# First attention of a fused attention and FFN kernel: next scores ahead of the values, a PSUM bank for the state sums, fewer dummy matmuls

## The reference

```
x = x + attention(layernorm(x), ctx, ctx)      # 16 heads of 32
x = x + ffn(layernorm(x))                      # 4-bit weights, 512 -> 2 x 1408 -> 512

# attention, per head: gates from [q, k, v]
log_D[s, t] = F[s] - F[t] + i[t]   for t <= s  # F: running sum of log-sigmoids
D  = exp(log_D - max_t log_D)
C  = (q @ k.T / sqrt(32)) * D
Cn = C / (max(|sum C|, exp(-max log_D)) + eps)
h  = Cn @ v, then normalized over the 32 of the head and scaled
```

## Time and profile before

| What | us |
|---|---|
| Median of 3 runs | 548.03 |
| Lowest and highest | 546.9, 548.43 |
| Profiled execution, its own time | 549.5 |
| Its span, first to last instruction | 547.8 |
| TensorE matmul busy | 507.3 (93%) |
| VectorE busy | 391.2 (71%) |
| GpSimd busy | 332.2 (61%) |
| ScalarE busy | 295.1 (54%) |
| Mean granted TensorE clock | 0.984 |

### The profile page before, as it was taken

The page is one execution under the profiler, slowest core; times in us unless marked ns, Lnnn a source line. Parts: engine busy times, 40 slices in busy tenths (PEclk is TensorE's granted clock), DMA queues, the critical chain, the costliest instruction groups (busy, mean ns, idle before and its releaser), DMA issues.

```text
span 547.8 us, 8218 instructions
## 1 busy us (share of the span) xinstructions
PE 507.3 (93%) x2752; PEld 280.2 (51%) x2752; DVE 391.2 (71%) x691; ACT 295.1 (54%) x639; POOL 332.2 (61%) x371
## 2 busy tenths in 40 slices
PE   0989996899999899999999999999999989989996
PEld 0556773436666345466665445566664443323442
DVE  4877878978888988277778898477778763877301
ACT  0355854387776352677767234787764224865000
POOL 1054446188887763667776883667768653888501
PEclk9988997999999999999999999999999999999999
DMA  8854037073103200456006001571000000200000
GB/s 270 245 175 167 9 109 256 33 258 136 40 2 134 97 0 2 130 186 225 0 7 227 0 1 41 193 269 39 2 1 1 19 20 25 90 1 1 20 19 38
DMA packets 22234, 47.81 MB, mean 87 GB/s; under 512 B 1840, under 2 KB 8880, under 8 KB 21680
## 3 DMA queue, kind: packets, MB, share of 16 engines
q1 hardware_dynamic: 22192, 47.28, 25.1%
HBM read 37.31 MB, written 4.33 MB: 76 GB/s over the span
## 4 chain that ended last, share of the span: by engine, by line
PE 73%; DVE 12%; ACT 5%; issue 4%; POOL 4%; DMA 1%; DVEq 0%; POOLq 0%; ACTq 0%
PE pf L993 25%; PE pf L979 18%; PE po L917 9%; PE pq L883 7%; PE pq L842 2%; PE pq L895 2%; PE pq L979 2%; PE pf L1012 2%; PE pq L922 2%; DVE ffn L1258 2%; ACT dmat L664 2%; DVE ffn L1262 1%; POOL hT L540 1%; ACT ts L698 1%; DVE bst L1081 1%
## 5 line engine op out<-in xcount | busy, mean ns | idle before, releaser
L993 PE MATMUL pf<-w_down,hT 128*128 128x512 f32 x352 | 154.0, 595 | 1.7 <-DVE w_down L1326 1.7
L979 PE MATMUL pf<-yT,gu_val 128*128 128x512 f16 x552 | 133.5, 380 | 4.5 <-DVE ffn L1262 1.7
L535 POOL TENSOR_TENSOR ffn<-ffn,ts 128x512 f32<-128x512 f32 x88 | 118.3, 1345 | 28.7 <-DVE ffn L1262 18.7
L698 ACT ACTIVATE ts<-pf,gu_scale 128x512 f32<-128x512 f32 x138 | 87.3, 684 | 46.8 <-PE pf L979 45.6
L993 PEld LDWEIGHTS pf<-w_down,hT 128*128 128x128 f32 x352 | 65.8, 190 | 83.8 <-issue 77.3
L979 PEld LDWEIGHTS pf<-yT,gu_val 128*128 128x128 f16 x552 | 49.9, 98 | 67.8 <-DVE ffn L1262 8.3
L664 ACT ACTIVATE dmat<-negm,aT 128x128 f32<-128x128 f32 x248 | 77.7, 396 | 0.8 <-DMA negm<-negm_dram 0.8
L540 POOL TENSOR_TENSOR hT<-ffn,th 128x512 f32<-128x512 f32 x44 | 57.7, 1314 | 28.9 <-DVE th L1271 28.9
L1258 DVE SCALAR_TENSOR_TENSOR ffn<-pf,gu_scale,ts 128x512 f32<-128x512 f32 x69 | 51.6, 748 | 32.7 <-PE pf L979 18.7
L917 PEld LDWEIGHTS po<-v_sb,dmat 128*128 128x128 f32 x512 | 62.1, 192 | 4.8 <-issue 0.4
L494 POOL TENSOR_SCALAR_AFFINE_SELECT dmat<-dmat 128x512 f32<-128x512 f32 x64 | 44.2, 705 | 27.1 <-ACT dmat L664 27.1
(11 more groups left out here) (124 smaller groups left out, 650.9 us busy)
## 6 DMA issues: line engine op xcount, KB each, us to landing
negm<-negm_dram SPq DMA_DIRECT2D x31, 512.0 KB, 5.2
ffn<-in_x SPq DMA_DIRECT2D x4, 1024.0 KB, 6.7
xT<-in_ctx_T SPq DMA_DIRECT2D x16, 256.0 KB, 6.0
ctx_sb<-in_ctx SPq DMA_DIRECT2D x4, 1024.0 KB, 5.7
x_sb<-in_x SPq DMA_DIRECT2D x4, 1024.0 KB, 5.5
x_res<-x_sb SPq DMA_DIRECT2D x4, 1024.0 KB, 5.4
out<-x_res SPq DMA_DIRECT2D x16, 256.0 KB, 2.2
ts<-in_gate_up_bytes SPq DMA_DIRECT2D x4, 352.0 KB, 9.5
```

Source lines behind the costliest of these rows:

```text
L535: pool.tensor_tensor(acc, acc, ts[:, h % TDEEP, 1], ALU.add).then_inc(tsum_ready, 1)
L698: act.activation(ts[:, h % TDEEP, g], bank(q, h, g), ACT.Copy, scale=gu_scale[:, g * GU + o:g * GU + o + 1]).then_inc(t_ready, 1)
L979: last = pe.matmul(bank(q, h, g), gu_val[:, h // 2 + h % 2 * FT, g], yT[:, part, g], start=(part == 0), stop=(part == 1))
L993: last = pe.matmul(pf[:, tt], hT[:, j, tt * P:(tt + 1) * P], w_down[:, j], start=(j == 0), stop=(j == FT - 1))
```

## The change

In the first attention, and only there:

- The second half of the next unit's scores is put directly behind the first half, both ahead of the values. The dummies that stood between the first half and the values are gone (six with unit 0, three with each of units 1 to 6). Those behind the state sums stay.
- The state sums of pair 0 go to `pf` bank 1, columns 0 to 131 (`bank_state`); the later part stays in `pq` bank 1. State sums now wait for `keep_state` of the unit before (`state_ready`), and the matmul L922 waits for the later part of the unit before (`later_ready`).
- On VectorE the later part of unit u is taken behind keep_state of unit u+1 (that of unit 7 at h = 17), ahead of the decode step.

```diff
+        def bank_state(p):
+            return pf[:, 1] if p == 0 else pq[:, 1]
...
                 pe.wait_ge(vw_ready, 2 * UNITS * p + 2 * u + 2)
-                if u > 0:
+                if p == 0:
+                    if u > 0:
+                        pe.wait_ge(state_ready, u)
+                elif u > 0:
                     pe.wait_ge(later_ready, UNITS * p + u)
                 elif q is not None:
                     pe.wait_ge(t_ready, 4 * FT * q + 2)
-                pe.matmul(pq[:, 1, 0:HG * (DH + 1)], ctx_sb[:, 2 * b, hg * P:(hg + 1) * P],
+                pe.matmul(bank_state(p)[:, 0:HG * (DH + 1)], ctx_sb[:, 2 * b, hg * P:(hg + 1) * P],
...
+                if p == 0 and u > 0:
+                    pe.wait_ge(later_ready, u)
                 pe.wait_ge(state_ready, UNITS * p + u + 1)
...
                         if q is None and s in VALUES and VALUES[s] + 1 < UNITS:
                             scores(p, q, VALUES[s] + 1, 0)
-                            if VALUES[s] == 0:
-                                keep_busy(6, po[:])
-                            else:
-                                keep_busy(3)
+                            scores(p, q, VALUES[s] + 1, 1)
                         if s in VALUES:
                             values(p, q, VALUES[s])
                             if q is None and VALUES[s] + 1 < UNITS:
-                                scores(p, q, VALUES[s] + 1, 1)
                                 state_sums(p, q, VALUES[s] + 1)
                                 keep_busy(6 if VALUES[s] == 0 else 3)
...
-                dve.tensor_tensor(state[:, u % 2], pq[:, 1, 0:HG * (DH + 1)].rearrange(
+                dve.tensor_tensor(state[:, u % 2], bank_state(p)[:, 0:HG * (DH + 1)].rearrange(
...
                     if u is not None and q is None:
                         products(p, u, range(BLKS))
                         keep_state(p, u)
+                        if u > 0:
+                            later_part(p, u - 1)
+                    if q is None and s - 1 in VALUES and VALUES[s - 1] == UNITS - 1:
+                        later_part(p, UNITS - 1)
...
-                    if p is not None and s in VALUES:
+                    if p is not None and q is not None and s in VALUES:
                         later_part(p, VALUES[s])
```

## The result

| | before | after |
|---|---|---|
| Median, us | 548.23 (546.9 to 548.55, 4 runs) | 563.22 (562.31 to 564.0, 4 runs) |
| Profiled execution, us | 549.5 | 562.63 |
| Span, us | 547.8 | 560.9 |
| Mean granted clock | 0.984 | 0.944 |

The ratio is 1.0278, with a 95% interval of 1.0252 to 1.0303: slower by 15.0 us. The forecast was 562, slower.

A forecast was written before the change was run, and what follows sets the result against it. TensorE's queue was taken to bound the first attention. First turn -3.4, full-clock units -0.6, five half-clock units +17.2 and the end about nothing gave +13, so 562 us; range 542.5 to 567, the forecast's own 554 to 567.

The forecast's parts named there:

- What bounds the loop, and the clock: First attention: TensorE's queue sets the pace at 5.12 us a unit; 3.9 us without dummies make its clock fall.
- unit 2 or 3: First attention loop: the units in which TensorE's clock was expected to fall to 1.2 GHz.
- The first turn, -3.4: Loop entry: products of unit 2 start at 46.9 in place of 50.33, a gain of 3.4 us.
- Units at half clock, 8.56: First attention loop: TensorE's unit takes 8.56 us at 1.2 GHz with values doubled, 3.44 more than now.
- B: First attention loop: the clock falls and comes back by turns; 549 to 554, say 551 us; chance 0.22.
- C: First attention loop: clock falls and stays at 1.2 GHz until the sixteen dummies behind unit 7; 562 us, chance 0.42.
- The end, "at about nothing": Loop end: the last unit's dummies and the end together change the time by about nothing.
- the sum: First attention: first turn -3.4, one or one and a half full-clock units -0.6, five half-clock units +17.2, end about nothing: +13.
- A: First attention loop: the clock holds at 2.4 GHz, -5.5 us; 544.0 profiled, 542.5 on the median; chance 0.28.
- VectorE's unit of 4.6: First attention, VectorE: products, state, decode, add and later part take 4.6 us a unit, without the 0.46 wait.
- D: First attention loop: scores ahead bring nothing, VectorE waits for state sums or weighted values; 545 to 549, say 548; chance 0.08.

The follow-up runs named there:

- run 4: Kernel before, with the 36 loop dummies from unit 1 on replaced by float32 matmuls of 33 columns: 571.58 us, ratio 1.0444.
- run 10: Kernel before, plus only eight dummies in TensorE's idle gap ahead of the first FFN products: 548.01 us, ratio 0.9998.
- run 1: Changed kernel with the removed dummies back, behind the second half of the scores (six with unit 0, three with units 1 to 6): 548.07 us, ratio 1.0005.
- run 5: Changed kernel with five dummies a unit: one between the score halves, two behind them, two behind the state sums (six with unit 0): 546.92 us, ratio 0.9983.
- run 2: Kernel before, old order and bank, only the dummies between first half of scores and values removed: 566.01 us, no ratio given.
- run 8: Kernel before, order and dummies kept, only the state sums' bank and the later part's place on VectorE changed: 548.89 us, ratio 1.0016.

## Why the prediction was right

**What bounds the loop, and the clock.** TensorE's queue set the pace and stayed the bound. The clock fell as the text had it, after a long time without a dummy (the first time at 40.7, earlier than its unit 2 or 3), and run 4 showed that it is narrow work in a full queue that loses it. The rule of the Trainium skill that was weighed (TensorE: Matmul & The Clock Gate, "Why this matters for your kernels"), that mid-kernel drops come with idle gaps, does not cover this case: the measurement decides, by 9.98 of 10.0 us busy ahead of the fall in run 4.

**The first turn, -3.4.** Products of unit 2 start 8.4 us behind those of unit 0, where 46.9 against 38.56 was 8.3. The size was right and its cause only in part: 1.6 of it was the half clock of the profiled execution of before, which not every execution has (run 10). At full clock the distance went from 10.15 to 8.63 (run 1) or 8.46 (run 5). As a gain over the median, 3.4 was about twice too much. This is probably the larger part of why run 1 came out at 548.07 and not at 546.

**Units at half clock, 8.56.** Measured 8.32: scores 2.45 (2.40 in the text), values 3.55 (3.42), L930 0.60 (0.62), state sums 0.44 (0.84), dummies 1.28. Doubling the values was right. The state sums were the one term off: the 0.42 of the earlier trace rows is theirs behind scores; behind the values, where the change puts them, the chain of run 1 has 0.23 at full clock, and 0.44 is that doubled. With it TensorE's unit of run 1 is 5.06 and not 5.3.

**Where the fall comes, and B against C.** The clock fell at 40.7, 47.5 and 54.2 and came back twice, as rival B had it, and then stayed low to the dummies behind unit 7, as C had it. With it the products of units 2 to 7 took 10.9 us more.

**The end, "at about nothing".** Taken alone it is not nothing. With the scores ahead, products of unit 7 start while the values of unit 6 have hardly begun (82.94 and 82.63), so two rounds of values at half clock still lie ahead of the head sums: 12.2 us from products to head sums instead of 7.7, +4.5. But the sum has this in its count. It takes one or one and a half units at full clock and five at half, six or more in all, and only five distances lie between the products of units 2 and 7. The 10.9 and the 4.5 belong together: 15.4 against 16.6.

**The term that was mis-sized.** The missing 1.2 goes back to the unit at half clock, which cost 3.20 us more than 5.12 and not 3.44; five times the difference is 1.2. In it the state sums are 0.40 too high, the scores and values 0.18 too low. Two things were in no term: the earlier start of the first products, -0.7, and the 1.6 behind the head sums, of which at least the last 0.7 have nothing to do with the change. Together they are +0.9 and nearly cancel the 1.2, so that 13.2 and 13.1 agree this well is luck. That the clock falls, stays low and makes the unit 1.6 times as long is not.

**The rivals.** A did not come about, and in the new order VectorE's unit of 4.6 was not reached even with the clock held. With enough dummies to hold it TensorE's own queue takes 5.06 (run 1), and with one less the weighted values are late in every other unit (run 5); the sum for A had put them at nothing. The old order did come to 4.6 while the clock held in run 2, with products at 48.05, 52.61 and 57.26. Of D, the wait for state sums is excluded by run 1: at full clock it was 0.2 us, once. The weighted values, which D named too, were late there by 0.5 in every unit.

## What to carry to other kernels

Dummies that hold TensorE's clock are part of the schedule. Before moving or cutting them, look for the stretches in which the clock fell in the present trace and ask what was in the queue, not if it was full. Put them where narrow matmuls would otherwise run for long, and into waits that exist anyway; a block of the same number in one place did not do. And take a stretch of time that one execution spent at half clock out of any gain that is read from it.

## What the runs showed of the hardware that was not expected

What stands ahead of a matmul changes its share of the chain: the same state sums take 0.42 us behind scores of 32 rows and 0.23 behind a matmul of 128 rows, here in run 1:

```profile
53.73 0.31 PE pq L930 x2
54.03 0.23 PE pf L901 x2
54.26 0.65 PE pf L1020 x3
```

The new bank is not the reason. In run 8 they go to it too, in the old order behind the scores:

```profile
58.00 0.64 PE pq L886 x8
58.64 0.42 PE pf L901 x2
```

And close to the edge the same program has two outcomes on one chip: 547.14 and 564.97 with four dummies a unit, 556.4 and 567.35 in run 2.
